# A graph attention and mixture-of-experts kernel: edges counted tile by tile, source one-hots begun on GpSimd, and other turns for weights, maxima and shifts

## The chip, the cores and the metric

The kernel runs on one core of a Trainium2 chip. The metric is the device time of one execution in microseconds. Engines are called by the profile's names: PE is TensorE (PEld its weight loads), DVE is VectorE, ACT ScalarE, POOL GpSimd, SP SyncE, which here only issues DMAs.

## The reference

1250 nodes of 768 values go through two graph attention layers, whose sum is added to x, and then through a mixture of eight experts with two chosen per node and a shared one. Edges are 21250 pairs (src, dst), sorted by dst; a self edge of each node is among them, and the reference adds one more.

```python
def _gat_layer(x, src, dst, W, a_src, a_dst, bias, concat):
    h = (x @ W).reshape(N, H, C)
    al_s = jnp.einsum('nhc,hc->nh', h, a_src)
    al_d = jnp.einsum('nhc,hc->nh', h, a_dst)
    e = jax.nn.leaky_relu(al_s[src] + al_d[dst], NEG_SLOPE)
    m = jax.ops.segment_max(e, dst, num_segments=N)
    ex = jnp.exp(e - m[dst])
    denom = jax.ops.segment_sum(ex, dst, num_segments=N)
    alpha = ex / (denom[dst] + 1e-16)
    out = jax.ops.segment_sum(h[src] * alpha[:, :, None], dst, num_segments=N)
...
x = x + gat(elu(gat(layernorm(x), W1, 4 heads of 512)), W2, 1 head of 768)
x = x + experts(layernorm(x))
```

## The kernel before

**Dense attention.** Edges are turned into a matrix of counts CT (1250 x 1250: how often src meets dst), kept as ten tiles of 125 sources. A softmax over edges is then one over a dense matrix: weight = count x exp(leaky(al_s + al_d) - shift), and aggregation is a matmul of h by these weights. Operands of the large matmuls are split in a high and a low 16-bit part (made by ScalarE and VectorE: `_hi` and `_lo`; GpSimd makes the low parts of W1 of head 0's last rows and of the experts), three products each.

**Stages**, each engine with its own hand-written order of instructions, held together by semaphores:

1. The x stage. VectorE turns src and dst into keys (chunk of dst, and source tile) that are laid out by four transposes on TensorE and copied to KEY and SLO (L1168, L1169). x comes in three pieces and is normalised (L1176 to L1193); TensorE transposes each of ten tiles (L1671), ScalarE and VectorE make its two parts (L896, L1220), and SyncE stores them to DRAM (xt_d), since SBUF holds three tiles only. W1's six row blocks for head 0 get their low parts at L1199.
2. The first projection (proj(0), L1654 in mm3): ten tiles of 18 matmuls. Each x tile is loaded back (L514). ScalarE copies a tile out of PSUM (L883), VectorE computes al_s and al_d from it (L1208) and the low part (L1213). Between the copies stand ScalarE's 32 sums for the second layer's attention vectors: GpSimd multiplies a block of W2's rows by att_src2 and att_dst2 (L774, two buffers) and ScalarE sums a product (L887, v2_sum). VectorE makes ten pieces of OL, the one-hots of sources within a tile (L1229, 2375 columns), in the same stretch. Then GpSimd works on W1 (L780, L781).
3. Counting (L1251 on VectorE, L1717 on TensorE). A loop of five turns, each with five chunks of 50 destinations: for every edge tile that may belong to a chunk VectorE makes a pair one-hot of 500 columns (12 buffers), and TensorE adds OL^T x one-hot into the chunk's PSUM bank; self edges are tiles of their own. 320 one-hots and matmuls. ScalarE copies each chunk to CT (L912). ScalarE also makes the high parts of head 1's W1 before its copies (L877). A total is checked at the end (L1259 to L1261); a wrong one would start a slow count of everything.
4. Masks: TensorE transposes CT's tiles (L1742), ScalarE turns counts into masks (two passes, L997 and L1000) and VectorE takes for every tile of destinations the maximum of al_s over its sources (L1299, chain_max); SyncE stores the masks (mask_d) for the later heads. The ten maxima become the softmax shifts (chain_shift: L1305 to L1309, a transpose on TensorE, L1698, a copy, L1314), go to DRAM (aa_d) and come back as rows. The first three tiles of the second projection are in this stage.
5. Four heads. Head h: the projection of head h+1 (ten tiles), then 15 groups: three blocks of destinations (500, 375, 375 columns), each with one denominator group and four aggregations (L1766, L1771), and for each the ELU and output (L1360 to L1386). A step of weights (p_steps) makes one source tile's weights in one block: ScalarE L925, L931, L943, VectorE L1320, L1328, L1335. Tables say how many steps stand in which tile of the projection (PJ_STEPS) and in which group (CUR_STEPS for this head, NEXT_STEPS for the next), where the ten maxima of the next head stand (MAX_STEPS), and where TensorE transposes and VectorE copies its shifts (SHIFT_AT). SyncE loads masks, W1 rows and x tiles for later heads in an order that is written out (L607 to L640).
6. The second layer, the router and the experts. GpSimd makes the low part of an expert's activations in three parts (L806); its down projection is L1654 in down().

```python
PJ_STEPS = [2, 1, 1, 0]
MAX_STEPS = [0, 0, 2, 2, 2, 2, 2, 0, 0, 0, 0, 0, 0, 0, 0]
ROW_AT, SHIFT_AT = 1, 8
```

## Time and profile before

| | us |
|---|---|
| median of 3 runs | 1466.32 |
| lowest and highest | 1466.25, 1472.4 |
| the profiled execution's own time | 1465.73 |
| its span in the trace | 1463.9 |
| TensorE busy | 1267.5 (87%) |
| VectorE busy | 931.5 (64%) |
| ScalarE busy | 595.6 (41%) |
| GpSimd busy | 257.6 (18%) |
| mean granted TensorE clock | 0.947 of full speed |

Busy is the time in which an engine executes; an engine may be idle or held for two reasons that this table doesn't tell apart, so the shares are to be read stage by stage. PE and DVE have 7118 and 1851 instructions in the trace. The largest group is TensorE's L1654 (projections and experts), 790.1 us busy.

### The profile page before, as it was taken

What the parts mean: (1) busy time and instruction counts of PE and PEld (TensorE: products, weight loads), DVE (VectorE), ACT (ScalarE), POOL (GpSimd) and SP (SyncE); (2) the same over time, 40 slices, a digit from 0 to 9 for tenths busy, and PEclk for the clock granted to TensorE, in tenths of its full rate; (3) what the DMA queues carried; (4) which work ended last, traced back from release to release, by engine and by line L of the source; (5) the groups of instructions that cost most, each with busy time, mean ns of one, the idle gap of its engine ahead of it and who ended that gap; (6) DMA issues with size and microseconds to landing.
All of it is one profiled execution on the core that took longest, in us unless ns stands there. A gap on an engine that the chain in (4) does not pass through costs nothing.

```text
span 1463.9 us, 19131 instructions
## 1 busy us (share of the span) xinstructions
PE 1267.5 (87%) x7118; PEld 814.8 (56%) x7118; DVE 931.5 (64%) x1851; ACT 595.6 (41%) x1025; POOL 257.6 (18%) x190
## 2 busy tenths in 40 slices
PE   1574898579599789979998999999999989999996
PEld 1342344334355455445456888888854746666664
DVE  6477997599788968988963456254478624333340
ACT  1344224566475546547842066200231134444441
POOL 1399300000000000000000000130011543443322
PEclk9987899899899989989998999999899989999999
DMA  8442201413441453114045611251310286767622
GB/s 209 153 161 76 78 0 34 144 51 95 114 131 38 113 157 90 40 36 117 30 134 187 187 58 57 75 149 32 97 66 1 62 240 175 187 174 173 164 58 29
DMA packets 71438, 152.66 MB, mean 104 GB/s; under 512 B 10837, under 2 KB 34901, under 8 KB 70730
## 3 DMA queue, kind: packets, MB, share of 16 engines
q1 hardware_dynamic: 64699, 134.28, 30.4%
q0 software_dynamic: 6656, 17.26, 6.1%
q8 instruction: 54, 0.88, 0.3%
q14 instruction: 29, 0.24, 0.1%
HBM read 118.93 MB, written 34.59 MB: 105 GB/s over the span
## 4 chain that ended last, share of the span: by engine, by line
PE 60%; DVE 17%; DMA 6%; ACT 6%; issue 5%; POOL 5%; SPq 1%; DVEq 0%; POOLq 0%; ACTq 0%
PE PS L1654 40%; PE PS L1771 10%; PE PS L1717 5%; DVE sb L1299 3%; POOL sb L774 3%; DVE sb L1320 2%; DVE sb L1328 2%; PE PS L1766 2%; DVE sb L1208 1%; DVE sb L1335 1%; DMA sb<-in_x_dram 1%; DVE sb L1251 1%; POOL sb L806 1%; DMA sb<-in_L_ffn_w_dram 1%; DVE sb L1371 1%
## 5 line engine op out<-in xcount | busy, mean ns | idle before, releaser
L1654 PE MATMUL PS<-sb,sb 128*125 128x384 f16 (+8 forms) x4404 | 790.1, 340 | 68.0 <-DVE sb L1213 23.4
L1654 PEld LDWEIGHTS PS<-sb,sb 128*125 128x125 f16 (+3 forms) x4404 | 543.7, 129 | 302.0 <-issue 70.7
L1771 PE MATMUL PS<-sb,sb 125*128 125x375 f16 (+1 forms) x1440 | 267.4, 347 | 0.0
L1771 PEld LDWEIGHTS PS<-sb,sb 125*128 125x128 f16 x1440 | 141.9, 99 | 121.9 <-issue 14.0
L786 POOL TENSOR_TENSOR sb<-sb,sb 125x768 f32<-125x768 f32 x10 | 18.0, 1841 | 784.4 <-DMA sb<-in_x_dram 784.4
L931 ACT ACTIVATE sb<-sb 125x375 f32<-125x375 f32 (+1 forms) x150 | 81.6, 544 | 116.1 <-DVE sb L1320 115.6
L1498 DVE SCALAR_TENSOR_TENSOR sb<-sb,sb 128x2304 f16<-128x2304 f32 x27 | 68.8, 2557 | 89.0 <-ACT sb L1066 89.0
L1717 PE MATMUL PS<-sb,sb 125*125 125x500 f16 x320 | 88.6, 417 | 12.6 <-DVE sb L1251 12.6
L1251 DVE TENSOR_SCALAR sb<-sb,sb 125x500 f16<-125x500 f16 x320 | 95.5, 380 | 3.3 <-PE PS L1717 3.2
L1320 DVE SCALAR_TENSOR_TENSOR sb<-sb,sb,sb 125x375 f32<-125x375 f32 (+1 forms) x150 | 95.3, 637 | 1.8 <-ACT sb L925 1.6
L925 ACT ACTIVATE sb<-sb,sb 125x375 f32<-125x375 f32 (+1 forms) x150 | 93.7, 628 | 3.9 <-DMA sb<-aa_d 3.9
L1208 DVE CUSTOM_DVE_ANT_0 sb<-PS,sb 125x512 f16<-125x512 f32 x80 | 55.2, 690 | 57.3 <-ACT sb L883 55.9
L1328 DVE SCALAR_TENSOR_TENSOR sb<-sb,sb 125x375 f32<-125x375 f32 (+1 forms) x150 | 87.6, 584 | 1.2 <-ACT sb L931 1.1
L1335 DVE TENSOR_TENSOR sb<-sb,sb 125x375 f16<-125x375 f32 (+1 forms) x150 | 87.8, 585 | 0.1
L774 POOL TENSOR_TENSOR sb<-sb,sb 128x768 f32<-128x768 f32 x32 | 77.9, 2469 | 55.6 <-DMA sb<-in_L_gnn_W_dram 46.6
L943 ACT ACTIVATE sb<-sb 125x375 f16<-125x375 f32 (+1 forms) x150 | 81.7, 545 | 8.5 <-DVE sb L1328 8.2
L1299 DVE CUSTOM_DVE_ANT_0 sb<-sb,sb 125x1250 bf16<-125x1250 bf16 x50 | 71.2, 1455 | 18.5 <-ACT sb L1000 10.0
L1717 PEld LDWEIGHTS PS<-sb,sb 125*125 x320 | 40.1, 141 | 60.9 <-issue 41.1
L806 POOL TENSOR_TENSOR sb<-sb,sb 128x392 f16<-128x392 f32 (+2 forms) x33 | 30.7, 931 | 203.3 <-ACT sb L1084 203.3
L1628 DVE TENSOR_TENSOR sb<-PS,sb 128x588 f16<-128x588 f32 x32 | 23.8, 767 | 66.5 <-ACT sb L1106 66.5
L1084 ACT ACTIVATE sb<-sb 128x392 f16<-128x392 f32 (+2 forms) x33 | 17.7, 536 | 108.6 <-DVE sb L1519 108.6
L968 ACT ACTIVATE sb<-sb,sb 128x375 f32<-128x375 f32 (+1 forms) x48 | 30.8, 641 | 69.7 <-DVE sb L1371 69.7
(190 smaller groups left out, 1122.8 us busy)
## 6 DMA issues: line engine op xcount, KB each, us to landing
sb<-in_L_ffn_w_dram SPq DMA_DIRECT2D x24, 1152.0 KB, 5.7
sb<-xt_d SPq DMA_DIRECT2D x40, 375.0 KB, 3.7
sb<-in_L_gnn_W_dram SPq DMA_DIRECT2D x32, 384.0 KB, 3.2
sb<-mask_d SPq DMA_DIRECT2D x20, 546.9 KB
sb<-h_d SPq DMA_DIRECT2D x10, 1000.0 KB, 5.5
h_d<-sb SPq DMA_DIRECT2D x16, 375.0 KB, 6.8
sb<-aa_d SPq DMA_DIRECT2D x5, 1093.8 KB
sb<-in_L_gnn_W_dram SPq DMA_DIRECT2D x18, 256.0 KB, 3.6
```

Of the source, the lines that this page charges most:

```text
L774: nc.gpsimd.tensor_tensor(VP[a][:, :], WV[ch % 3][:, :], A2R[:, a, :], ALU.mult).then_inc(s_vp, 1)
L925: A(TMP[:, q % NTMP, 0:n], ROW[:, 1, lo:lo + n], ACT.Identity, bias=ALF[:, h, i:i + 1]).then_inc(s_p1, 1)
L931: A(TMP[:, q % NTMP, 0:n], TMP[:, q % NTMP, 0:n], ACT.Exp).then_inc(s_p3, 1)
L943: A(P[:, i, 0, lo:lo + n], TMP[:, q % NTMP, 0:n], ACT.Copy).then_inc(s_p5, 1)
L1251: V.tensor_scalar(OR[:, n % RO, :], iok[:, :], 1000.0 * c, KEY[:, bass.ds(col, 1)], ALU.add, ALU.is_equal).then_inc(s_or, 1)
L1299: V.tensor_tensor_reduce(junk, mask, max_row(h), 1.0, 3.0 * NEG, ALU.add, ALU.max, MX[:, j:j + 1]).then_inc(s_mu, 1)
L1320: V.scalar_tensor_tensor(TMP[:, q % NTMP, 0:n], ROW[:, 0, lo:lo + n], AL[:, 0, h, i:i + 1], TMP[:, q % NTMP, 0:n], ALU.add, ALU.max).then_ ...
L1328: V.scalar_tensor_tensor(TMP[:, q % NTMP, 0:n], TMP[:, q % NTMP, 0:n], 1.0, CT[:, i, lo:lo + n], ALU.min, ALU.mult).then_inc(s_p4, 1)
L1335: V.tensor_tensor(P[:, i, 1, lo:lo + n], TMP[:, q % NTMP, 0:n], P[:, i, 0, lo:lo + n], ALU.subtract).then_inc(s_p6, 1)
L1654: ins = M(out_, lhs(a), rhs(b), start=first and a + b == 0, stop=last and a == 1)
L1717: ins = M(PS[0:T, c, 0:KC], OL[:, bass.ds(col, 1), :], OR[:, n % RO, :], start=q == 0, stop=q == len(jobs[c]) - 1)
L1771: ins = M(PS[:, t, 0:n], hb[:, i, pa, 128 * c:128 * c + 128], P[:, i, pb, lo:lo + n], start=i == 0 and pa + pb == 0, stop=i == NT - 1 and ...
```

## The change

- **Counting by tiles.** For each of the 170 edge tiles the one or two chunks that it may meet are listed (`met`); VectorE makes the one-hots for both in one operation of 500 or 1000 columns (170 of them), TensorE adds into four PSUM banks in turn (286 matmuls), with no loop. Self edges are no tiles any more: two VectorE operations add the identity to CT's diagonal blocks. 24 tiles (39 matmuls) are counted between the transposes of x. There are 8 one-hot buffers for 12.
- **Source one-hots.** GpSimd subtracts (ten operations of 2250 columns, the last of 1125, from 9.5 us on), VectorE compares with zero in place.
- **The products for W2's attention vectors** stand behind these: ten on GpSimd, then the low parts of W1, then 22 more; four buffers for two. ScalarE has six of the sums in the first projection, sixteen between chunk copies (three for four chunks) and ten in tile 3 of the second projection, all at once. The split of the sums (v2_split) moves to head 0's fifth group.
- **The first projection** takes x's tiles in the order 7, 8, 9, 0 to 6, and the first three aren't loaded back. The load of head 1's W1 rows is spread over this.
- **Masks** are made in one ScalarE pass; VectorE subtracts them.
- **The heads.** New tables: in heads 0 and 1 three steps of weights per group first, the ten maxima from group 5 to 9, the shifts at group 12 for 8; in head 2 shifts at 10. h1's stores stand ahead of the shift rows on SyncE, and one W1 load behind them.
- **Experts.** Each expert's first down projection waits part by part.

```diff
+    reach = [(max(0, c * DC * NE // N - MARGIN) // T, min(ET, -(-((c + 1) * DC * NE // N + MARGIN) // T)))
+             for c in range(NC)]
+    met = [[c for c in range(NC) if reach[c][0] <= t < reach[c][1]] for t in range(ET)]
+    assert all(1 <= len(m) <= 2 for m in met)
```
```diff
-        PJ_STEPS = [2, 1, 1, 0]
-        CUR_STEPS = [[3, 3, 2, 2, 2, 2, 2, 2, 0, 0, 0, 0, 0, 0, 0],
-                     [2, 2, 2, 2, 2, 2, 2, 0, 0, 0, 0, 0, 0, 0, 0],
-                     [2, 2, 2, 2, 2, 2, 2, 0, 0, 0, 0, 0, 0, 0, 0],
+        PJ_STEPS = [[0, 0, 0, 0, 2, 2, 2, 2, 2, 2], [1] * NT, [1] * NT]
+        CUR_STEPS = [[3, 3, 3, 3, 3, 2, 2, 1, 0, 0, 0, 0, 0, 0, 0],
+                     [3, 3, 3, 3, 3, 2, 2, 1, 0, 0, 0, 0, 0, 0, 0],
+                     [3, 3, 2, 2, 2, 2, 2, 2, 2, 0, 0, 0, 0, 0, 0],
                      [3, 3, 3, 3, 2, 2, 2, 0, 0, 0, 0, 0, 0, 0, 0]]
-        MAX_STEPS = [0, 0, 2, 2, 2, 2, 2, 0, 0, 0, 0, 0, 0, 0, 0]
-        NEXT_STEPS = [[0, 0, 0, 0, 0, 0, 0, 0, 0, 0, 1, 2, 2, 2, 2],
-                      [0, 0, 0, 0, 0, 0, 0, 0, 0, 0, 1, 2, 2, 2, 2],
-                      [0, 0, 0, 0, 0, 0, 0, 0, 0, 0, 2, 2, 3, 3, 3]]
+        MAX_STEPS = [[0, 0, 0, 0, 0, 2, 2, 2, 2, 2, 0, 0, 0, 0, 0],
+                     [0, 0, 0, 0, 0, 2, 2, 2, 2, 2, 0, 0, 0, 0, 0],
+                     [0, 0, 2, 2, 2, 2, 2, 0, 0, 0, 0, 0, 0, 0, 0]]
+        NEXT_STEPS = [[0, 0, 0, 0, 0, 0, 0, 0, 0, 0, 0, 0, 0, 0, 2],
+                      [0, 0, 0, 0, 0, 0, 0, 0, 0, 0, 0, 0, 0, 0, 2],
+                      [0, 0, 0, 0, 0, 0, 0, 0, 0, 0, 0, 3, 3, 3, 3]]
...
-        W1_AT = {3: 0, 4: 1, 5: 2, 6: 3, 7: 4, 8: 5}
-        ROW_AT, SHIFT_AT = 1, 8
+        W1_AT = {6: 0, 7: 1, 10: 2, 11: 3, 12: 4, 13: 5}
+        ROW_AT, SHIFT_AT = 1, [12, 12, 10]
```
SyncE, start and heads:
```diff
+            sp.wait_ge(s_xT, NT)
             sp.dma_start(A2R[:, 0, :], as2.to_broadcast([128, D])).then_inc(s_a2v, 16)
             sp.dma_start(A2R[:, 1, :], ad2.to_broadcast([128, D])).then_inc(s_a2v, 16)
-            for i in range(NT):
-                store_xt(i)
             for ch in range(3):
                 load_v2(ch)
-            for i in range(NT):
-                load_xt(0, i)
-                load_v2(3 + i)
-            for ch in range(3 + NT, NCH):
+            for q in range(3, NT):
+                load_xt(0, q)
+            load_w1_rows(1, range(2))
+            for ch in range(3, 8):
                 load_v2(ch)
+            load_al(1)
...
-            load_w1(1)
-            sp.wait_ge(s_vp, 2 * NCH)
             chain_row(0)
+            load_w1_rows(1, range(2, KD))
             for i in range(3):
                 load_xt(1, i)
+            for ch in range(8, NCH):
+                load_v2(ch)
...
                     load_masks(h + 1, 3)
                     load_masks(h + 1, 4)
+                    store_h1(NB * h)
                     if h + 2 < H:
-                        load_w1_rows(h + 2, range(2, KD))
+                        load_w1_rows(h + 2, range(2, 5))
                     chain_shift(h + 1)
+                    if h + 2 < H:
+                        load_w1_rows(h + 2, range(5, KD))
```
GpSimd and ScalarE:
```diff
+            pool.wait_ge(s_slo, 1)
+            for i in range(NT):
+                a, b = OLP * i, min(OLP * (i + 1), KA)
+                nc.gpsimd.tensor_tensor(OL[:, a:b, :], iot[:, :].unsqueeze(1).to_broadcast([T, b - a, T]),
+                                        SLO[:, a:b].unsqueeze(2).to_broadcast([T, b - a, T]), ALU.subtract
+                                        ).then_inc(s_od, 1)
...
+                        k = 2 * ch + a
+                        if k >= 4:
+                            pool.wait_ge(s_va, k - 3)
+                        nc.gpsimd.tensor_tensor(VP[k % 4][:, :], WV[ch % 3][:, :], A2R[:, a, :], ALU.mult
+                                                ).then_inc(s_vp, 1)
...
                 h_hi(0, i)
-                while k * NT < 2 * NCH * (i + 1):
-                    v2_sum(k)
-                    k += 1
-            act.sem_inc(s_ce, 1)
+                if i >= 4:
+                    v2_sum(summed)
+                    summed += 1
             w1_hi(1, range(KD))
...
+            for c in range(NC):
+                act.wait_ge(s_cm, reach[c][1])
+                A(CT[:, :, c * DC:c * DC + DC], PS[0:T, c % 4, 0:KC].rearrange("p (i n) -> p i n", n=DC), ACT.Copy,
+                  accum_out=CS[:, c:c + 1]).then_inc(s_ce, 1)
+                if c >= 4 and c % 4 < 3:
+                    v2_sum(summed)
+                    summed += 1
...
-                  ACT.Relu, bias=1.0, scale=-1.0).then_inc(s_act, 1)
-                act.wait_ge(s_act, j + 1)
-                A(MSK[:, j % 2, :], MSK[:, j % 2, :], ACT.Copy, scale=NEG).then_inc(s_mm, 1)
+                  ACT.Relu, bias=big[:, :], scale=NEG).then_inc(s_mm, 1)
...
+                        if h == 0 and i == NT // 3:
+                            for k in range(summed, 2 * NCH):
+                                v2_sum(k)
```
VectorE (the code of before at L1229 and L1251 is taken out):
```diff
+            def source_onehots(q):
+                a, b = OLP * q, min(OLP * (q + 1), KA)
+                dve.wait_ge(s_od, q + 1)
+                V.tensor_scalar(OL[:, a:b, :], OL[:, a:b, :], 0.0, None, ALU.is_equal).then_inc(s_ol, 1)
+
+            def pair_onehots(tiles):
+                for t in tiles:
+                    if t >= RO and t % RG == 0:
+                        dve.wait_ge(s_cm, t - RO + RG)
+                    c, w = met[t][0], len(met[t])
+                    V.tensor_scalar(OR[:, t % RO, 0:w, :], iok[:, 0:w, :], float(SP * c), KEY[:, t:t + 1], ALU.add,
+                                    ALU.is_equal).then_inc(s_or, 1)
+
+            piece(0)
+            piece(1)
+            for i in range(XF):
+                xt_lo(i)
+                if i < 2:
+                    source_onehots(i)
+                pair_onehots(range(T0 * i // XF, T0 * (i + 1) // XF))
+            piece(2)
+            for i in range(XF, NT):
+                xt_lo(i)
+
+            for q in range(NT):
+                h_lo(0, q)
+                if q >= 2:
+                    source_onehots(q)
...
+            pair_onehots(range(T0, ET))
+            dve.wait_ge(s_ce, NC)
...
+            flat = CT[:, :, :].rearrange("p i n -> p (i n)")
+            own = flat[:, 0:(NT - 1) * (N + T)].rearrange("p (i n) -> p i n", n=N + T)[:, :, 0:T]
+            V.tensor_tensor(own, own, idh[0:T, 0:T].unsqueeze(1).to_broadcast([T, NT - 1, T]), ALU.add
+                            ).then_inc(s_ctok, 1)
+            own = flat[:, (NT - 1) * (N + T):NT * N]
+            V.tensor_tensor(own, own, idh[0:T, 0:T], ALU.add).then_inc(s_ctok, 1)
```
TensorE:
```diff
+            def counts(tiles):
+                for t in tiles:
+                    if t % OLP == 0:
+                        pe.wait_ge(s_ol, t // OLP + 1)
+                    if t % PG == 0:
+                        pe.wait_ge(s_or, min(t + PG, ET))
+                    for w, c in enumerate(met[t]):
+                        if t == reach[c][0] and c >= 4:
+                            pe.wait_ge(s_ce, c - 3)
+                        ins = M(PS[0:T, c % 4, 0:KC], OL[:, t, :], OR[:, t % RO, w, :], start=t == reach[c][0],
+                                stop=t == reach[c][1] - 1)
+                    ins.then_inc(s_cm, 1)
+
+            def early(i):
+                return 2 * (T0 * i // XF // 2)
+
+            for i in range(XF):
+                x_T(i)
+                if i >= 2:
+                    counts(range(early(i - 2), early(i - 1)))
+            counts(range(early(XF - 2), T0))
+            for i in range(XF, NT):
+                x_T(i)
...
+            def down(lhs, wb, o_, made=None):
                 for q in range(2):
                     for m in range(KI):
+                        if made is not None and q == 0:
+                            pe.wait_ge(s_sg, made + KI)
+                            pe.wait_ge(s_alo, made + m + 1)
+                        elif made is not None:
+                            pe.wait_ge(s_gx, made + KI)
```

How the order of instructions changes, at three places. VectorE before, from SLO's copy to the first tile of the first projection (sb_52 is x, sb_190 and sb_191 its statistics, sb_69 the transposed x, sb_70 W1's parts, sb_51 is OL):

```order
L1169 COPY sb_149<-PS 125x170
...
L1193 TENSOR_SCALAR sb_52<-sb_52,sb_191,sb_165 125x768 x5
L1220 TENSOR_TENSOR sb_69<-PS,sb_69 128x750 x5
L1199 SCALAR_TENSOR_TENSOR sb_70<-sb_53,sb_70 128x512
L1220 TENSOR_TENSOR sb_69<-PS,sb_69 128x750
...
L1229 TENSOR_TENSOR sb_51<-sb_147,sb_149 125x2375
L1208 ISA sb_54,sb_156<-PS,sb_72 125x512
```

And with the change (x is sb_78, the transposed x sb_67, OL sb_51, the pair one-hots sb_59, W1 sb_68):

```order
L1188 COPY sb_153<-PS 125x170
L1189 COPY sb_152<-PS 125x170
...
L1214 TENSOR_SCALAR sb_78<-sb_78,sb_81,sb_169 125x768 x3
L1242 TENSOR_TENSOR sb_67<-PS,sb_67 128x750
L1251 TENSOR_SCALAR sb_51<-sb_51 125x2250
L1258 TENSOR_SCALAR sb_59<-sb_150,sb_152 125x500 x4
L1242 TENSOR_TENSOR sb_67<-PS,sb_67 128x750
L1251 TENSOR_SCALAR sb_51<-sb_51 125x2250
L1258 TENSOR_SCALAR sb_59<-sb_150,sb_152 125x1000 x5
...
L1258 TENSOR_SCALAR sb_59<-sb_150,sb_152 125x500
L1196 BN_STATS sb_80<-sb_78 125x6 x10
```

OL's compare has moved from the first projection between x's low parts, and pair one-hots stand behind it, ahead of x's last five tiles.

TensorE before, from x's transposes (L1671) to the row of al_s (L1694), with the loop of counting behind it:

```order
L1671 MATMUL PS<-sb_139,sb_52 128x125 x60
L1654 MATMUL PS<-sb_70,sb_69 125x512 x180
L1694 MATMUL PS<-sb_139,sb_156 10x125
L1708 UNCONDITIONAL_BRANCH
L1708 ISA
L1716 ISA
L1717 ISA
L1717 MATMUL PS<-sb_61,sb_51 125x500
```

And with the change (L1705 transposes, L1718 counts, L1688 projects, L1753 the row):

```order
L1705 MATMUL PS<-sb_143,sb_78 128x125 x18
L1718 MATMUL PS<-sb_59,sb_51 125x500 x4
L1705 MATMUL PS<-sb_143,sb_78 128x125 x6
L1718 MATMUL PS<-sb_59,sb_51 125x500 x8
L1705 MATMUL PS<-sb_143,sb_78 128x125 x6
L1718 MATMUL PS<-sb_59,sb_51 125x500 x27
L1705 MATMUL PS<-sb_143,sb_78 128x125 x30
L1688 MATMUL PS<-sb_68,sb_67 125x512 x180
L1753 MATMUL PS<-sb_143,sb_160 10x125
L1718 MATMUL PS<-sb_59,sb_51 125x500 x247
```

39 matmuls of counting have moved between the transposes, and 247 stand behind the projection.

SyncE in head 0 before, around the next head's shift rows (L560 and L566), with masks (L555), W1 (L481), h1 (L575) and x (L514):

```order
L481 DMA sb_71<-in_L_gnn_W_dram 128x512 x4
L560 DMA aa_d<-sb_162 20x125
L566 DMA sb_62<-aa_d 112x2500
L566 DMA sb_62<-aa_d 13x2500
L555 DMA sb_65<-mask_d 112x2x1250
L555 DMA sb_65<-mask_d 13x2x1250
L555 DMA sb_64<-mask_d 112x2x1250
L555 DMA sb_64<-mask_d 13x2x1250
L575 DMA h_d<-sb_75 128x4x500 x2
L514 DMA sb_69<-xt_d 128x1500 x3
L575 DMA h_d<-sb_76 128x3x500 x2
```

And with the change (shift rows L567 and L573, masks L562, W1 L490, h1 L582, x L519):

```order
L582 DMA h_d<-sb_73 128x4x500 x2
L490 DMA sb_69<-in_L_gnn_W_dram 128x512 x3
L567 DMA aa_d<-sb_166 20x125
L573 DMA sb_60<-aa_d 112x2500
L573 DMA sb_60<-aa_d 13x2500
L490 DMA sb_69<-in_L_gnn_W_dram 128x512
L562 DMA sb_63<-mask_d 112x2x1250
L562 DMA sb_63<-mask_d 13x2x1250
L562 DMA sb_62<-mask_d 112x2x1250
L562 DMA sb_62<-mask_d 13x2x1250
L519 DMA sb_67<-xt_d 128x1500 x3
L582 DMA h_d<-sb_74 128x3x500 x2
```

The first store pair of h1 stands ahead of the shift rows, and one W1 load behind them.

## Rows read from the trace of the kernel before

**Rows 1.** Windows of the whole run: stretch, us, busy (x) by engine, PEclk, DMA share, GB/s:
```profile
49.50:137.70 88.20, 49.23 (x180) 28.16 (x180) 57.05 (x61) 32.13 (x69) 74.78 (x31) 0.85 0.36 120
137.70:241.90 104.20, 89.31 (x323) 40.46 (x323) 97.58 (x329) 22.83 (x62) 19.44 (x14) 0.90 0.12 37
241.90:286.30 44.40, 29.62 (x188) 19.89 (x189) 24.11 (x50) 25.96 (x25) 0.00 (x0) 0.85 0.46 134
...
325.40:418.00 92.60, 76.90 (x419) 41.06 (x420) 82.75 (x144) 57.56 (x113) 0.00 (x0) 0.91 0.39 109
418.00:460.40 42.40, 40.36 (x181) 23.83 (x180) 36.23 (x79) 21.77 (x43) 0.00 (x0) 1.00 0.27 82
460.40:553.60 93.20, 81.55 (x447) 43.16 (x446) 77.42 (x134) 50.66 (x98) 0.00 (x0) 0.93 0.39 108
...
596.10:694.70 98.60, 86.45 (x468) 45.00 (x467) 84.16 (x148) 57.42 (x112) 0.00 (x0) 0.95 0.25 69
```

**Rows 2.** Timeline of PE, start, us, line, what, [idle before, releaser]: L1698:
```profile
381.07 0.38 PE L1698 MATMUL PS<-sb,sb 125*20 125x125 f32 x1 [15.70 <-DVE sb L1308]
...
516.05 0.38 PE L1698 MATMUL PS<-sb,sb 125*20 125x125 f32 x1 [11.63 <-DVE sb L1308]
```

**Rows 3.** Source view of L774, GpSimd's groups by form, VectorE's timeline at 8 us:
```profile
L774 POOL TENSOR_TENSOR sb<-sb,sb x26: 1794/1808/4202, 53.9 to 123.9; 128x768 f32<-128x768 f32 x26
...
L806 POOL TENSOR_TENSOR sb<-sb,sb 128x392 f16<-128x392 f32 x24 | 22.2, 926 | 118.0 <-ACT sb L1084 118.0
...
L781 POOL TENSOR_TENSOR sb<-sb,sb 128x512 f16<-128x512 f32 x6 | 6.9, 1152 | 0.5
...
9.47 0.34 DVE L1169 COPY sb<-PS 125x170 f32<-125x170 f32 x1
```

**Rows 4.** Source views of L1251 and L1489, and GpSimd in the timeline there:
```profile
L1251 DVE TENSOR_SCALAR sb<-sb,sb x3: 339/695/1892, 138.5 to 140.9; 125x500 f16<-125x500 f16 x3
...
139.01 1.85 POOL L774 TENSOR_TENSOR sb<-sb,sb 128x768 f32<-128x768 f32 x1
...
L1489 DVE TENSOR_SCALAR sb<-sb,sb,sb x10: 678/678/2198, 953.6 to 1047.1; 125x768 f32<-125x768 f32 x10
```

**Rows 5.** Timeline near 1145 us: one-hots on VectorE, additions on GpSimd:
```profile
1144.84 4.71 DVE L1602 TENSOR_SCALAR sb<-sb,sb 125x392 bf16<-125x392 f16 x20
...
1146.23 8.52 POOL L816 TENSOR_TENSOR sb<-sb,sb 125x768 f32<-125x768 f32 x3 [7.07 <-ACT sb L1097]
```

**Rows 6.** Groups by form in counting, 187 to 240 us:
```profile
L1251 DVE TENSOR_SCALAR sb<-sb,sb 125x500 f16<-125x500 f16 x191 | 49.8, 344 | 1.3 <-PE PS L1717 1.3
```

**Rows 7.** ScalarE: timeline of L877, and groups by form 50 to 131 us:
```profile
158.61 0.63 ACT L877 ACTIVATE sb<-sb 128x512 f16<-128x512 f32 x1 [2.19 <-DMA sb<-in_L_gnn_W_dram]
...
L887 ACT ACTIVATE sb<-sb 128x768 f32<-128x768 f32 x27 | 22.7, 842 | 33.0 <-POOL sb L774 33.0
```

**Rows 8.** VectorE's groups by form, 460 to 600 us (busy, mean ns, idle before):
```profile
L1208 DVE CUSTOM_DVE_ANT_0 sb<-PS,sb 125x512 f16<-125x512 f32 x22 | 15.2, 691 | 7.1 <-ACT sb L883 6.7
L1299 DVE CUSTOM_DVE_ANT_0 sb<-sb,sb 125x1250 bf16<-125x1250 bf16 x10 | 14.2, 1454 | 0.0
L1320 DVE SCALAR_TENSOR_TENSOR sb<-sb,sb,sb 125x375 f32<-125x375 f32 x21 | 12.4, 590 | 0.0
...
L1320 DVE SCALAR_TENSOR_TENSOR sb<-sb,sb,sb 125x500 f32<-125x500 f32 x10 | 7.2, 721 | 0.1
```

**Rows 9.** Head 1's shift rows and the x load behind: timeline and source L514:
```profile
523.67 0.27 DVE L1314 COPY sb<-PS 20x125 f32<-20x125 f32 x1
...
533.12 1.31 ACT L925 ACTIVATE sb<-sb,sb 125x500 f32<-125x500 f32 x2 [0.41 <-DMA sb<-aa_d]
...
L514 SPq DMA_DIRECT2D sb<-xt_d x1: 3196/3196/3196, 529.2 to 529.2; - x1
...
DMA to landing us min/median/max: 14.1/14.1/14.1
```

**Rows 10.** Timeline of PE, an expert's down projection:
```profile
1276.66 2.64 PE L1654 MATMUL PS<-sb,sb 128*98 128x384 f16 x15 [1.28 <-POOL sb L806]
```

265 lines of the change are left out of this document (109 added, 156 removed).

## The prediction

> **What bounds the kernel now.** I first cut the profiled execution into stages by a table of windows (core busy time per stretch), then read, for each stage, which wait ends last. The columns to compare are the length of a stretch with its TensorE busy time [rows 1]: the x stage ends at 49.5 us; the first head's projection takes 88.2 us for 49.2 us of TensorE work; counting and its check take 104.2 us; the mask stage up to the first weights 44.4 us; the attention of heads 0, 1 and 2 takes 92.6, 93.2 and 98.6 us. From counting on VectorE is as busy as TensorE in these stretches. The projection is slow because ScalarE's sums for W2 stand in its queue between the copies that free PSUM, behind GpSimd products of 1.8 us and their loads; counting is at VectorE's pace. Two of the attention stretches hold one gap each, where TensorE stands at the transpose of the next head's shifts until VectorE has made ten maxima: 15.7 and 11.6 us [rows 2].
>
> **The lock that the change leans on.** The change gives GpSimd ten differences of 2250 columns (the last 1125). GpSimd's tensor_tensor takes 1.80 us for 768 columns, 1.15 for 512 and 0.93 for 392 [rows 3], so 2.25 to 2.36 ns a column, and I take 5.1 us for 2250 (from 4.4, the slope between the 392 and 512 columns of its two 16-bit forms, up to 5.8). What this does to VectorE shows in three rows: while such an operation of 1.85 us runs, one of three pair one-hots takes 1892 ns, which are 344 on the mean elsewhere [rows 4, 6], and the operation that normalises a tile of 768 columns takes 2.20 us in one case of ten instead of 0.68 [rows 4]. So VectorE's SBUF-to-SBUF tensor_scalar waits until GpSimd's operation has ended. Conversely, twenty one-hots in a dense row (4.71 us) kept a GpSimd addition waiting: two additions, 3.6 us by their length [rows 3], took 6.75 [rows 5].
>
> **The x stage.** SLO is copied at 9.5 us [rows 3] and GpSimd starts. VectorE is then let in about once per GpSimd operation, with a group of adjacent instructions. I lay them out: the 2 normalisations (1.3 us) behind the first difference, 3 (2.0) behind the second, then source one-hots with 4 pair one-hots (1.8), with 5 (2.6), 5 (1.7), 5 (1.7), W1's low part with 5 (2.5), and the last 5 normalisations (3.0): 16.6 us in the port. 9.5 + 9.5 x 5.1 + 16.6 = 74.6; five more low parts of x and W1, two passes of about 0.69 [rows 8] together, give 82 us in place of 49.5: **+32.5**. The one-hots are priced from counting: 191 of 500 columns fill 49.8 us [rows 6], 0.26 each, where twenty of 392 columns take 0.235 each [rows 5]: 0.13 per 500 columns on a fixed 0.13, so 0.39 for 1000.
>
> **The first projection.** Nothing but six sums stands in it now; three tiles of x need no reload. A tile then takes 4.2 us (ten in 42.4 [rows 1]); with a slow first tile of 6 and 2.6 for the last copy and low part it ends at 82.3 + 6 + 9 x 4.25 + 2.6 = 129 instead of 137.7. The stage goes from 88.2 to 47.4: **-40.8**.
>
> **Counting.** The order shows a wait that counting did not have: ScalarE makes the high parts of W1 for head 1 before its first chunk copy, and TensorE, which has four banks, stops at tile 25 for that copy. Before, the last of these parts was made at 158.6 us [rows 7], 24 us after the projection, beside the first five chunks. GpSimd now also has a product to finish, and SyncE the row's round trip: I take 19.4 us from the end of the projection, nearly all with TensorE idle. Then 247 matmuls stay (286 in all, 39 early). TensorE needs some 0.2 us each (447 of 375 to 512 columns in 81.55 [rows 1]), 50 us. VectorE needs 101 x 0.39 for the tiles that meet two chunks and 45 x 0.26 for the rest, less 8 tiles that it makes ahead in the gap: 48. But sixteen W2 products of 1.8 us are tied in by ScalarE's sums, one for three chunks of four, and take the port; I let twelve to fifteen cost VectorE their length: 48 + 22 to 27 = 70 to 75, and take 70. The diagonal and the check I put at 4.4 us. 19.4 + 70 + 4.4 = 93.8 in place of 104.2: **-10.4**.
>
> The Trainium skill (SBUF — State Buffer, Who interferes with whom) says that whoever issues first holds the pair of ports that VectorE and GpSimd share for the whole instruction, and the other fully blocks. By that rule a GpSimd operation that is already queued goes ahead of VectorE's next one, and the sum would be rival (b)'s, 1467. Rows 4 agree with the blocking; rows 5, where GpSimd's operation waited through a row of one-hots, speak against the turns.
>
> **Masks and head 0.** One ScalarE pass per mask falls away. VectorE's ten maxima (1.45) and three tiles' low parts (three passes of 0.69) are 20.7 us [rows 8]; I take 24.5 from the transposes to the last maximum for 31.3: **-7**. Then ScalarE has ten sums of 842 ns [rows 7] behind six products of 1.8: about 12.9 us before the next copy out of PSUM. The wait for the shift rows, which was there anyway, covers about half: tile 4's copy comes 6 us later. The pipe of weights now fills only after it (2), and since tile 3 makes no steps any more the tenth tile's weights come two steps later (4): **+12**.
>
> **Attention, heads 0 and 1.** A step of weights on VectorE is three passes, 1.46 us in 375 columns and 1.85 in 500 (the first pass: 0.59 and 0.72), two maxima 2.8, a y about 1.7 [rows 8]. Three steps a group first, then maxima: the shifts are ready some 79 us after the projection in head 0 and 71 in head 1, and TensorE meets them at group 12, with 5 to 6 us of wait left and 3 us before the third block's weights. By adding groups: 83 us for 92.6 in head 0, **-9.6**, and 87.5 for 93.4 in head 1, **-5.9**. Head 2's projection runs its steps in 500 columns instead of 375, 0.3 us more a tile: **+1.8**, and so head 3's: **+1.8**.
>
> What is late next is a load. SyncE issues the x tiles of the projection after next behind the shift rows and two pairs of masks. After head 1's shift copy at 523.67 the first x tile was issued at 529.2 and took 14.1 us to land [rows 9], 19.6 us in all, with 1 MB of h1 ahead of it that the change moves away: about 16.5. The copy can only come once group 12 is read, 10.5 us before group 14 ends. So TensorE waits some 6 us for x before the projections of heads 2 and 3: **+12** together.
>
> **Head 2.** Its shifts move two groups, but its next head's weights can't start before the rows are back, 9.4 us after the copy (533.12 for 523.67 [rows 9]). With 20 own steps in nine groups VectorE ends these at 66 us; the copy follows group 10's reciprocal, 70; rows at 79.4; ten tiles' first weights take 28 us after that, as they did. Head 3's first denominator ends at 107.6 instead of 98.6: **+9**.
>
> **Experts.** TensorE waited 1.28 us at each expert's down projection for GpSimd's last low part [rows 10]; now the first two of three parts start before it, six matmuls, 1.0 us of cover, eight times: **-7.8**. The other moved loads, the h1 stores among them, cost nothing: SyncE reaches them while TensorE is in the same head's groups, and where that cover goes is the load wait above.
>
> **Sum.** +32.5 - 40.8 - 10.4 - 7 + 12 - 9.6 - 5.9 + 3.6 + 12 + 9 - 7.8 = -12.4. The span of 1463.9 becomes 1451.5, the execution's 1465.7 becomes 1453.3. The median shown is 0.6 above that execution, so I say **1454 us**.
>
> **The rivals.** (a) GpSimd's differences don't shut VectorE out: their 18 rows of 125 let it in between, or 16-bit columns go faster. For it: no row has such a form, and GpSimd's 1.5 us tensor_scalar let one-hots through. Against: rows 4. The x stage then ends at about 54 us: 1454 - 28 = 1426, and where also the products yield in counting (-15), 1411. (b) GpSimd and VectorE take turns instruction by instruction; the one-hots of 1892 and 695 ns [rows 4] can be read so. Then VectorE makes one instruction per difference, ten of some forty, and x ends at 95: 1454 + 13 = 1467, no change. This is what the rule of the Trainium skill told above would make of the stage. (c) Slower: the differences cost much more than 2.3 ns a column, for their broadcast rows. Each microsecond on each of them puts 9.5 us on the x stage, all of it on the path. From 7.2 us each it is slower by over 0.5%; at 8, 1454 + 28 = 1482. Nothing in the trace shows a broadcast on GpSimd. (d) The heads cost less than I add: x tiles land in time and head 2 is not held, 1454 - 21 = 1433.
>
> **Chances.** A difference of 0.5%, 7 us, is about what a measurement of this kernel can tell from none: the three runs span 6. My forecast 0.42, (a) 0.24, (b) 0.12, (c) 0.10, (d) 0.12. My own case lies within 15 us of 1454, mostly below 1459. Faster 0.72 (all of (a) and (d), most of mine), the same 0.15, slower 0.13. The range leaves out the far end of (a) and most of (c): **1410 to 1475**; the forecast's own is 1439 to 1469.
>
> **What would show it.** Right: TENSOR_TENSOR of 125x2250 on GpSimd near 5 us; a normalisation or one-hot of several microseconds in the x stage; its last low part near 82 us; TensorE idle some 18 us after tile 24, released by ScalarE's copy; 125x1000 one-hots at 0.39 pitch, and slower with a product beside them; the shift gaps down to about 5 us; a gap before the projections of heads 2 and 3 released by the x tile's load; a gap of about 16 us in head 3's first denominator; 32.1 us an expert instead of 33.1. Wrong: the x stage ending before 60 (then (a)) or after 100 ((c)); no load wait in the heads ((d)); counting at 50 us after its gap, which means that the products do not lock VectorE out.

## The result, and the profile after

The changed kernel takes 1473.41 us (median of 20 runs, 1466.82 to 1482.39) against 1466.74 of the kernel before (20 runs, 1464.29 to 1474.97): a ratio of 1.0038, 95% interval 1.0022 to 1.0055. That is 6.7 us slower, where I had forecast 1454, 12 us faster. It stays inside the half per cent that I had called the same (a chance of 0.15), and inside my range, but on the other side of the kernel before. The profiled execution took 1474.92 us, its span is 1473.2, the mean granted clock 0.933 (0.947 before). The experiments below were measured in three later series, each beside the kernel before, whose medians there were 1468.88, 1469.18 and 1470.85 us. A ratio in brackets is against the kernel before of the same series. "Less than the changed kernel" is a plain difference to 1473.41 from the first series, and leaves out this drift of 2 to 4 us. So small differences are read from stages of the traces instead.

This table of windows of the changed kernel has the columns of [rows 1]; its stretches are the same stages, cut where TensorE begins them:

```profile
0.00:79.30 79.30, 24.55 (x103) 17.24 (x103) 70.72 (x100) 12.68 (x20) 43.12 (x30) 0.92 0.46 121
79.30:123.20 43.90, 41.01 (x180) 25.37 (x180) 26.67 (x58) 11.95 (x24) 18.12 (x10) 0.95 0.54 164
123.20:145.30 22.10, 1.36 (x3) 0.37 (x3) 6.80 (x10) 3.08 (x7) 14.74 (x12) 0.52 0.52 155
145.30:223.90 78.60, 59.74 (x247) 34.64 (x247) 68.71 (x142) 29.10 (x80) 52.29 (x18) 0.91 0.13 40
223.90:251.30 27.40, 20.57 (x155) 15.40 (x155) 21.26 (x40) 14.32 (x13) 0.00 (x0) 0.81 0.52 149
251.30:310.20 58.90, 39.35 (x147) 21.06 (x148) 34.76 (x69) 35.01 (x65) 10.65 (x6) 0.82 0.28 80
310.20:397.20 87.00, 79.25 (x419) 41.62 (x417) 71.84 (x128) 45.52 (x92) 0.00 (x0) 0.93 0.31 85
397.20:403.50 6.30, 0.00 (x0) 0.00 (x0) 4.05 (x7) 4.88 (x10) 0.00 (x0) 0.78 1.05 274
403.50:455.70 52.20, 46.58 (x200) 26.82 (x201) 38.76 (x80) 23.41 (x42) 0.00 (x0) 0.96 0.27 86
455.70:543.90 88.20, 79.61 (x427) 41.74 (x425) 71.61 (x125) 45.31 (x91) 0.00 (x0) 0.94 0.32 84
543.90:550.90 7.00, 0.07 (x2) 0.05 (x1) 3.52 (x7) 4.54 (x9) 0.00 (x0) 0.76 1.04 278
550.90:603.00 52.10, 46.51 (x201) 26.65 (x202) 39.28 (x82) 23.98 (x44) 0.00 (x0) 0.96 0.28 81
603.00:704.40 101.40, 87.63 (x448) 42.85 (x447) 89.25 (x157) 63.67 (x126) 0.00 (x0) 0.89 0.23 68
...
781.00:1227.10 446.10, 424.24 (x2656) 325.06 (x2655) 227.91 (x526) 116.80 (x185) 65.66 (x47) 0.95 0.33 99
1227.10:1473.20 246.10, 232.59 (x1482) 157.46 (x1482) 80.89 (x68) 102.27 (x119) 91.92 (x77) 0.98 0.57 142
```

Measured against the stages of before, cut at the same instructions, in the order of the forecast's terms (stage before, after, difference, forecast):

| stage | before | after | moved | forecast |
|---|---|---|---|---|
| x stage | 49.5 | 79.3 | +29.8 | +32.5 |
| projection 0 | 88.2 | 43.9 | -44.3 | -40.8 |
| counting and check | 104.2 | 100.7 | -3.5 | -10.4 |
| masks to the shifts | 32.3 | 27.4 | -4.9 | -7 |
| to head 0's attention | 51.2 | 58.9 | +7.7 | +12 |
| attention 0 | 92.4 | 87.0 | -5.4 | -9.6 |
| waits for x, heads 2 and 3 | 0 | 13.3 | +13.3 | +12 |
| projection 2 and first denominator | 46.8 | 52.2 | +5.4 | +1.8 |
| attention 1 | 89.0 | 88.2 | -0.8 | -5.9 |
| projection 3 and first denominator | 46.9 | 52.1 | +5.2 | +1.8 |
| attention 2 and denominator 3 | 94.1 | 101.4 | +7.3 | +9 |
| head 3 | 76.4 | 76.6 | +0.2 | 0 |
| second layer, router | 439.3 | 446.1 | +6.8 | 0 |
| experts | 253.5 | 246.1 | -7.4 | -7.8 |

At the masks the changed kernel is 18.0 us ahead (223.9 for 241.9), as the forecast had it (18.7). It keeps that lead until the first wait for x, ahead of head 2's projection, and has lost it, and more, when the second layer begins (781.0 for 771.1).

### The profile page after: what moved, and what is told of

The parts are those of the page before. It is cut to its first block, busy times and chain, and to the rows that moved or that the text cites. A ratio compares the mean times of both kernels' runs of the same rounds, so it can differ in the third digit from the quotient of the medians.

```text
span 1473.2 us, 18197 instructions
## 1 busy us (share of the span) xinstructions
PE 1259.6 (86%) x7084; PEld 817.3 (55%) x7084; DVE 916.0 (62%) x1694; ACT 584.3 (40%) x1015; POOL 296.5 (20%) x198
## 4 chain that ended last, share of the span: by engine, by line
PE 52%; DVE 24%; ACT 6%; DMA 6%; issue 6%; POOL 5%; SPq 1%; POOLq 0%; DVEq 0%; ACTq 0%
PE PS L1688 39%; PE PS L1816 8%; DMA sb<-in_L_gnn_W_dram 3%; DVE sb L1258 3%; DVE sb L1230 3%; DVE sb L1352 3%; DVE sb L1331 3%; POOL sb L784 2%; DVE sb L1360 2%; DVE sb L1367 1%; DVE sb L1214 1%; DVE sb L1235 1%; ACT sb L965 1%; PE PS L1718 1%; DMA sb<-in_L_ffn_w_dram 1%
## 5 line engine op out<-in xcount | busy, mean ns | idle before, releaser
L1688 PE MATMUL PS<-sb,sb 128*125 128x384 f16 (+8 forms) x4404 | 789.5, 339 | 54.2 <-DVE sb L1235 17.3
L1688 PEld LDWEIGHTS PS<-sb,sb 128*125 128x125 f16 (+3 forms) x4404 | 545.0, 130 | 285.7 <-issue 68.4
L1816 PE MATMUL PS<-sb,sb 125*128 125x375 f16 (+1 forms) x1440 | 272.3, 351 | 0.0
L1352 DVE SCALAR_TENSOR_TENSOR sb<-sb,sb,sb 125x375 f32<-125x375 f32 (+1 forms) x150 | 95.9, 640 | 13.6 <-ACT sb L947 13.5
L1718 PE MATMUL PS<-sb,sb 125*125 125x500 f16 x286 | 70.5, 402 | 38.1 <-ACT sb L932 23.4
L1258 DVE TENSOR_SCALAR sb<-sb,sb 125x1000 f16<-125x1000 f16 (+1 forms) x170 | 81.4, 555 | 21.7 <-PE PS L1718 21.7
L1331 DVE CUSTOM_DVE_ANT_0 sb<-sb,sb 125x1250 bf16<-125x1250 f32 x50 | 71.2, 1456 | 14.5 <-ACT sb L1019 4.9
L1811 PE MATMUL PS<-sb,sb 125*128 125x375 f16 (+1 forms) x240 | 52.4, 362 | 30.3 <-DVE sb L1367 30.3
L1718 PEld LDWEIGHTS PS<-sb,sb 125*125 125x125 f16 x286 | 40.0, 146 | 67.3 <-ACT sb L932 24.6
L990 ACT ACTIVATE sb<-sb,sb 128x375 f32<-128x375 f32 (+1 forms) x48 | 30.8, 642 | 78.6 <-DVE sb L1403 78.6
```

What stands on the lines that cost most here:

```text
L1258: V.tensor_scalar(OR[:, t % RO, 0:w, :], iok[:, 0:w, :], float(SP * c), KEY[:, t:t + 1], ALU.add, ALU.is_equal).then_inc(s_or, 1)
L1331: V.tensor_tensor_reduce(junk, max_row(h), mask, 1.0, 3.0 * NEG, ALU.subtract, ALU.max, MX[:, j:j + 1]).then_inc(s_mu, 1)
L1352: V.scalar_tensor_tensor(TMP[:, q % NTMP, 0:n], ROW[:, 0, lo:lo + n], AL[:, 0, h, i:i + 1], TMP[:, q % NTMP, 0:n], ALU.add, ALU.max).then_ ...
L1688: ins = M(out_, lhs(a), rhs(b), start=first and a + b == 0, stop=last and a == 1)
L1718: ins = M(PS[0:T, c % 4, 0:KC], OL[:, t, :], OR[:, t % RO, w, :], start=t == reach[c][0], stop=t == reach[c][1] - 1)
L1816: ins = M(PS[:, t, 0:n], hb[:, i, pa, 128 * c:128 * c + 128], P[:, i, pb, lo:lo + n], start=i == 0 and pa + pb == 0, stop=i == NT - 1 and ...
```

## What the traces show of the two halves

**The x stage: turns, not groups.** GpSimd's ten differences, a source view, with minimum, median and maximum in ns:

```profile
L773 POOL TENSOR_TENSOR sb<-sb,sb x10: 2383/3944/4259, 9.5 to 45.9; 125x2250 f16<-125x2250 f16 x9, 125x1125 f16<-125x1125 f16 x1
```

And VectorE's timeline beside them (start, us, line, what):

```profile
13.96 3.44 DVE L1207 TENSOR_SCALAR sb<-sb 125x2 f32<-125x2 f32 x1
17.44 8.48 DVE L1214 TENSOR_SCALAR sb<-sb,sb,sb 125x768 f32<-125x768 f32 x2
25.84 2.85 DVE L1196 BATCH_NORM_STATS2 sb<-sb 125x6 f32<-125x384 f32 x6
...
33.69 12.70 DVE L1214 TENSOR_SCALAR sb<-sb,sb,sb 125x768 f32<-125x768 f32 x3
46.31 0.93 DVE L1242 TENSOR_TENSOR sb<-PS,sb 128x750 f16<-128x750 f32 x1
47.16 1.76 DVE L1251 TENSOR_SCALAR sb<-sb 125x2250 f16<-125x2250 f16 x1
48.84 1.12 DVE L1258 TENSOR_SCALAR sb<-sb,sb 125x500 f16<-125x500 f16 x4
```

The differences take 3.9 us on the median, 1.8 ns a column, less than even my lower bound of 4.4, and run without a break to 48.3 us. Each of VectorE's SBUF-to-SBUF tensor_scalars waits for one of them: even the one of two columns (L1207) takes 3.44, the two and three normalisations (L1214, 0.68 each when alone) 8.48 and 12.70. That is one operation to a difference. What doesn't wait is as plain: statistics (L1196, six in 2.85) and the low part that reads PSUM (L1242, 0.93) have their own length. From 48.8 us on four one-hots take 1.12 together. So the mechanism was rival (b)'s, and my layout in groups was wrong; the stage still ended near my 82 us only because two errors cancelled: the differences were shorter than I took them, and all of the one-hots came behind them. That is luck.

**Counting: the other way round.** The same two engines between 158 and 203 us; VectorE's row is its one-hots, GpSimd's a W2 product:

```profile
158.65 27.21 DVE L1258 TENSOR_SCALAR sb<-sb,sb 125x1000 f16<-125x1000 f16 x73
```

```profile
166.42 21.09 POOL L784 TENSOR_TENSOR sb<-sb,sb 128x768 f32<-128x768 f32 x1 [6.04 <-ACT sb L907]
```

Here VectorE's 73 one-hots ran in a dense row of 27.2 us, 0.37 each, the length that they have alone. One product, which takes 1.8 when alone, took 21.1 and ended 1.7 us after the row. Then it was ScalarE's turn to be late, and TensorE's (timelines; the brackets are idle time before, and the releaser):

```profile
187.54 0.84 ACT L907 ACTIVATE sb<-sb 128x768 f32<-128x768 f32 x1 [9.75 <-POOL sb L784]
```

```profile
145.34 8.99 PE L1718 MATMUL PS<-sb,sb 125*125 125x500 f16 x35 [19.18 <-ACT sb L932]
...
189.10 5.49 PE L1718 MATMUL PS<-sb,sb 125*125 125x500 f16 x17 [4.19 <-ACT sb L932]
```

ScalarE stood 9.75 us for that product with a chunk's copy behind it in its queue, and TensorE 4.2 us for the copy. Now the held products come at once, and the engines take turns again: between 190.6 and 202.4 us GpSimd made seven products and VectorE seven one-hots, one to one, in 12.1 us where such a row alone needs 2.7. The 19.18 us in the first PE row are the forecast's wait (19.4) for W1's high parts.

The Trainium skill (SBUF — State Buffer, Who interferes with whom) has the first to issue hold the shared ports for the whole instruction, where VectorE's operation needs both pairs. The trace agrees in the x stage, where each tensor_scalar waits out a difference. The same section lets an operation with one SBUF input, outside the modes that use both ports, run free, and the statistics agree. In counting the product was the one kept out, over dozens of VectorE's operations that were issued after it, and this the rule does not tell.

**The heads.** TensorE's timeline:

```profile
378.44 0.38 PE L1757 MATMUL PS<-sb,sb 125*20 125x125 f32 x1 [5.25 <-DVE sb L1340]
...
403.53 17.78 PE L1688 MATMUL PS<-sb,sb 128*125 128x512 f16 x72 [6.38 <-issue]
...
444.64 4.07 PE L1688 MATMUL PS<-sb,sb 128*125 128x512 f16 x18 [0.50 <-DVE sb L1235]
...
455.12 0.81 PE L1811 MATMUL PS<-sb,sb 125*128 125x500 f16 x2 [2.61 <-DVE sb L1367]
...
525.26 0.38 PE L1757 MATMUL PS<-sb,sb 125*20 125x125 f32 x1 [6.92 <-DVE sb L1340]
...
550.88 9.45 PE L1688 MATMUL PS<-sb,sb 128*125 128x512 f16 x35 [6.93 <-issue]
```

The waits at the shifts (L1757) fell from 15.7 and 11.6 us [rows 2] to 5.3 and 6.9, and that of head 2, 8.8 us in the trace of before, is gone. In their place stand 6.4 and 6.9 us ahead of the projections, a pause of 0.50 in nearly every tile (before, the last six tiles of a projection ran without one), and 2.6 us inside the first denominator, whose last weights come out of that projection. In head 2 the next head's first denominator trickles in one pair of matmuls at a time; one of its waits:

```profile
688.40 0.60 PE L1811 MATMUL PS<-sb,sb 125*128 125x500 f16 x2 [1.67 <-DVE sb L1367]
```

The experts do as forecast, 0.40 where there were 1.28 [rows 10], in 32.21 us each for 33.12:

```profile
1259.33 2.12 PE L1688 MATMUL PS<-sb,sb 128*98 128x384 f16 x12 [0.40 <-POOL sb L821]
```

## The experiments

**heads_before** and **heads_alone** split the change in two.

```diff
-        PJ_STEPS = [[0, 0, 0, 0, 2, 2, 2, 2, 2, 2], [1] * NT, [1] * NT]
+        PJ_STEPS = [[2] * NT, [1] * NT, [1] * NT]
...
-        ROW_AT, SHIFT_AT = 1, [12, 12, 10]
+        ROW_AT, SHIFT_AT = 1, [8, 8, 8]
...
-                        load_w1_rows(h + 2, range(2, 5))
+                        load_w1_rows(h + 2, range(2, KD))
                     chain_shift(h + 1)
```

(all five tables are as before, the sixth W1 row is no longer loaded behind the shift rows, and store_h1 stands behind the shift rows and ahead of the x loads, as before; heads_alone puts the same difference the other way into the kernel before, except for head 0's steps in tile 3 of its projection)

> The changed kernel with the five step tables, the shift groups and SyncE's order in the heads as before; counting, masks, projection order and experts stay changed. Theory A: the start gains (223.9 for 241.9 us at the masks, 251.3 for 274.2 at head 0's shifts) and the experts gain 7.4; what is lost lies in the heads from the second projection's end to head 3's first denominator, where the new turns cost 25 us in all (att of head 0 +0.8, projections +5.4 and +5.2, head 1 +6.2, head 2 +7.2). So about 1474 - 25 = 1449, below the kernel before by 17. Rival B: the heads are slower because the start leaves something behind them (a lower granted clock, 0.933 for 0.947; late sums), whatever the tables: then 1468 to 1474.

> The kernel before with only the new step tables, shift groups and SyncE's order in the heads. Theory A: slower than before by about 25 us, 1491, with a gap of 6 to 7 us before the projections of heads 2 and 3, 4.56 us for most tiles in them, and a slower head 2. Rival B: within 3 us of before.

Measured: heads_before 1456.25 us (ratio 0.9908, interval 0.9874 to 0.9942), heads_alone 1490.04 (1.0151, 1.01 to 1.0202). The new turns, with SyncE's new order, are what loses: 17 us from one side (25 were expected), 21 from the other. Rival B is out, since the old turns are 17 us faster behind the very same start, at the same clock (0.935). In heads_before TensorE has the old picture, no pause in the last six tiles and the long waits at the shifts:

```profile
368.11 0.38 PE L1753 MATMUL PS<-sb,sb 125*20 125x125 f32 x1 [16.27 <-DVE sb L1336]
...
423.99 25.07 PE L1684 MATMUL PS<-sb,sb 128*125 128x512 f16 x108 [0.37 <-DVE sb L1231]
```

and in heads_alone the new one:

```profile
416.33 18.75 PE L1658 MATMUL PS<-sb,sb 128*125 128x512 f16 x72 [6.72 <-issue]
...
468.88 0.60 PE L1770 MATMUL PS<-sb,sb 125*128 125x500 f16 x2 [2.61 <-DVE sb L1339]
```

**x_first** and **x_w1_first** mend SyncE's order.

```diff
                     store_h1(NB * h)
                     if h + 2 < H:
-                        load_w1_rows(h + 2, range(2, 5))
+                        for i in range(3):
+                            load_xt(h + 2, i)
+                        load_w1_rows(h + 2, range(2, KD))
                     chain_shift(h + 1)
-                    if h + 2 < H:
-                        load_w1_rows(h + 2, range(5, KD))
```

(x_w1_first; x_first moves the x tiles alone; in both the x tiles' old load, further down, is taken out)

> The changed kernel, with the three x tiles that SyncE loads behind the shift rows and two pairs of masks issued ahead of the W1 rows and the shift rows instead. Theory A: the two gaps before the projections of heads 2 and 3 (6.4 and 6.9 us, named issue in the trace) go, and with them the low clock at each projection's start: 13 to 15 us less, 1459 to 1461. Rival C: the gaps have another cause that stands behind the same load (ScalarE's W1 part behind the shift rows, whose wait of 4.4 us is in the same place): then 2 us or less.

> As x_first (1461.95), and W1's sixth row block is loaded ahead of the shift rows too, where the kernel before had it. Theory A: in x_first the gap before the projections of heads 2 and 3 shrank from 6.4 and 6.9 us to 1.8 and 1.2, released by VectorE's last low part of W1, whose load came late, and ScalarE stood 3.8 us for that load; both go: 3 to 6 us less, 1456 to 1459, and so within 3 us of heads_before (1456.25), which means that the new turns are worth nothing in heads 0 and 1 even with their loads in time. Rival I: the tables were only spoiled by the two loads: below 1452.

Measured: x_first 1461.95 (0.9953, 0.993 to 0.9975), 11.5 less than the changed kernel; x_w1_first 1458.59 (0.9893, 0.9838 to 0.9947), 3.4 less again. In x_first the wait before head 2's projection is down to 1.8 us and has another releaser, VectorE's low part of W1, behind a ScalarE that waits for the row's load:

```profile
404.56 7.98 PE L1687 MATMUL PS<-sb,sb 128*125 128x512 f16 x36 [1.81 <-DVE sb L1219]
```

```profile
403.16 0.63 ACT L895 ACTIVATE sb<-sb 128x512 f16<-128x512 f32 x1 [3.83 <-DMA sb<-in_L_gnn_W_dram]
```

In x_w1_first that is gone too. Whether it is worth 3.4 us isn't shown. From the transpose of head 0's shifts to the first matmul of the second layer the changed kernel's trace has 529.7 us, x_first 513.1, x_w1_first 514.1 and heads_before 509.9. In another place the same code differs by more: counting behind its first wait took 84.9 us in x_first's trace and 79.1 in x_w1_first's.

These stretches say what the new turns lose: of the 19.8 us between the changed kernel and heads_before the two late loads make 15.6, and the tables themselves 4.2. The tables do gain where they were meant to: with the loads in time attention 0 takes 86.4 us for heads_before's 94.7, and attention 1 88.1 for 89.8. They lose 5.0 and 3.3 in the projections of heads 2 and 3 with their first denominators, and 6.5 behind these. Rival I, below 1452, isn't borne out, though one of the four runs took 1450.61 and the interval reaches below it.

**max_early** asks whether the place of the maxima makes the wait at the shifts.

```diff
-        MAX_STEPS = [[0, 0, 0, 0, 0, 2, 2, 2, 2, 2, 0, 0, 0, 0, 0],
-                     [0, 0, 0, 0, 0, 2, 2, 2, 2, 2, 0, 0, 0, 0, 0],
+        MAX_STEPS = [[0, 0, 2, 2, 2, 2, 2, 0, 0, 0, 0, 0, 0, 0, 0],
+                     [0, 0, 2, 2, 2, 2, 2, 0, 0, 0, 0, 0, 0, 0, 0],
```

> The changed kernel with the next head's maxima in groups 2 to 6 instead of 5 to 9 in heads 0 and 1; steps and shift group stay. Theory A: TensorE's wait at the shifts (5.3 and 6.9 us) is not there because the maxima are late as such but because VectorE has 28 steps, ten maxima and the outputs of eight groups ahead of group 12 and is paced by ScalarE in the groups with maxima. With the maxima earlier the shifts are ready before group 12 but the own weights of blocks two and three come later: the wait moves to their denominators and the time stays within 4 us. Rival G: the maxima's place alone makes the wait; it goes and 10 us with it, 1463.

Measured: 1471.88 (1.0023, 1.0003 to 1.0042), within 2 us of the changed kernel. The wait at the shifts is gone in both heads. In head 0 the third block's denominator has two waits of 3.2 us instead, and the x load comes no earlier:

```profile
370.89 0.81 PE L1811 MATMUL PS<-sb,sb 125*128 125x375 f16 x2 [3.17 <-DVE sb L1367]
...
378.99 0.27 PE L1757 MATMUL PS<-sb,sb 125*20 125x125 f32 x1
...
402.77 18.22 PE L1688 MATMUL PS<-sb,sb 128*125 128x512 f16 x72 [7.63 <-issue]
```

The wait moves to the denominators, as Theory A has it, and Rival G's 10 us are not there. But the place of the maxima isn't without effect. Attention 0 and 1 take 84.5 and 84.0 us here, for 87.0 and 88.2 in the changed kernel's trace, and the waits for x behind them grow from 6.4 and 6.9 us to 7.6 and 9.1. So half of the 6.7 us gained goes into the late load, which hides it from the total.

**w1_later** takes the wait ahead of counting.

```diff
-            w1_hi(1, range(KD))
...
                   accum_out=CS[:, c:c + 1]).then_inc(s_ce, 1)
+                if c < KD:
+                    w1_hi(1, (c,))
```

> The changed kernel with ScalarE's six high parts of head 1's W1 each behind one of the first six chunk copies, not all ahead of the first. Theory A: TensorE's 19.2 us wait at tile 25 goes, but VectorE's one-hots then meet GpSimd's six low parts (1.17 us each) as well as the products, and VectorE sets the pace: 8 to 12 us less, 1462 to 1466. Rival D: counting is bound by the sums and products in ScalarE's queue, so that the wait only moves to a later chunk: 3 us or less.

Measured: 1464.31 (0.9972, 0.9949 to 0.9994), 9.1 less, so Rival D falls. In the traces the masks begin 5.5 us earlier (218.4 for 223.9) and the second layer 6.2; the rest lies where the code is the same. The wait of 19.2 us is gone from tile 25; the longest in counting is now this, where a chunk's copy stands behind a W1 row that is still being loaded:

```profile
149.83 7.67 PE L1718 MATMUL PS<-sb,sb 125*125 125x500 f16 x21 [7.66 <-ACT sb L930]
```

**ol_dve** and **diff_small** are about the differences.

```diff
-                V.tensor_scalar(OL[:, a:b, :], OL[:, a:b, :], 0.0, None, ALU.is_equal).then_inc(s_ol, 1)
+                V.tensor_tensor(OL[:, a:b, :], iot[:, :].unsqueeze(1).to_broadcast([T, b - a, T]),
+                                SLO[:, a:b].unsqueeze(2).to_broadcast([T, b - a, T]), ALU.is_equal
+                                ).then_inc(s_ol, 1)
```

(ol_dve; GpSimd's ten subtractions are taken out)

> The changed kernel without GpSimd's ten differences: VectorE makes the source one-hots itself in one operation (2.6 us for 2375 columns in the kernel before) in the places where it now compares with zero. Theory A, the lock: the x stage ends near 62 us for 79, the first projection gets 5 us longer because eight of the longer operations stand in it (2.1 + 2.5 us of VectorE a tile), the sum is 10 to 13 us less, 1461 to 1464. Rival E: the differences cost VectorE nothing and the x stage is long for its own one-hots: then the stage ends near 84 and the time goes up by 5.

```diff
+                for lo in range(a, b, 6):
+                    hi = min(lo + 6, b)
+                    ins = nc.gpsimd.tensor_tensor(OL[:, lo:hi, :], iot[:, :].unsqueeze(1).to_broadcast([T, hi - lo, T]),
...
+                ins.then_inc(s_od, 1)
```

(diff_small; the operation over all columns is taken out)

> The changed kernel with each of GpSimd's ten differences cut into three of 750 columns (the same columns in all). Theory J, turns: between 9.5 and 48.3 us VectorE got one SBUF tensor_scalar in for each of the ten differences, so with 29 shorter ones it gets three times the turns: its 9 early operations are through at about 9.5 + 9 x 1.4 + their own length = 28 us, TensorE's transposes start by 16 and 20 us, and the x stage ends 15 to 20 us earlier, near 62: 1455 to 1459. Theory A of the forecast, groups: VectorE takes all that stands ready whenever GpSimd ends an operation, so the number of operations matters as well, but it would have been through with 9 in five turns: 3 to 8 us less. Rival K: GpSimd keeps the port until its queue is empty, whatever the cut: no change, 1473.

Measured: ol_dve 1454.99 (0.9898, 0.9851 to 0.9946), 18.4 less; diff_small 1470.88 (1.0002, 0.9978 to 1.0025), 2.5 less, or 5 by the ratios, whose intervals just touch. In ol_dve the transposes start at 13.45 us and the projection at 57.7 for 79.35; its tiles wait 0.41 for the longer operation of VectorE:

```profile
13.45 2.76 PE L1701 MATMUL PS<-sb,sb 125*128 125x125 f32 x12 [4.59 <-DVE sb L1208]
...
57.70 25.69 PE L1684 MATMUL PS<-sb,sb 128*125 128x512 f16 x108 [2.46 <-DVE sb L1214]
...
97.09 4.07 PE L1684 MATMUL PS<-sb,sb 128*125 128x512 f16 x18 [0.41 <-DVE sb L1229]
```

```profile
L1245 DVE TENSOR_TENSOR sb<-sb,sb 125x2250 f16<-125x2250 f16 x9 | 25.5, 2830 | 0.0
```

Rival E falls. The 21.6 us that the x stage gives are more than my 17, and the projection pays about 7 of them back; at the masks ol_dve is 14.7 us ahead (209.3 for 223.9). The rest of the 18.4 isn't placed. diff_small shows the turns operation by operation, and that I had overrated them:

```profile
14.14 3.46 DVE L1216 TENSOR_SCALAR sb<-sb,sb,sb 125x768 f32<-125x768 f32 x2
...
30.15 5.85 DVE L1260 TENSOR_SCALAR sb<-sb,sb 125x500 f16<-125x500 f16 x4
...
37.81 7.94 DVE L1260 TENSOR_SCALAR sb<-sb,sb 125x1000 f16<-125x1000 f16 x5
```

Its transposes begin at 15.95 and 17.66 us, as turns foretold (16 and 20). But the one-hots, which had stood behind the last difference, now stand beside the differences, and each took a turn as well: four in 5.85 us and five in 7.94, which need 1.12 and 2.03 otherwise. GpSimd's 29 pieces end at 54.0 us, the projection begins at 76.8, 2.6 us earlier. What VectorE gains by shorter turns it pays by more of them. Rival K's reason is out, since the transposes did start earlier; of theory J only the mechanism holds. The total can't tell these 2.6 us: in this trace counting behind its first wait took 85.0 us for 78.6, with the same code.

**small_products** cuts the products of W2.

```diff
-                        nc.gpsimd.tensor_tensor(VP[k % 4][:, :], WV[ch % 3][:, :], A2R[:, a, :], ALU.mult
+                        w = D if k < 4 else 8
+                        nc.gpsimd.tensor_tensor(VP[k % 4][:, 0:w], WV[ch % 3][:, 0:w], A2R[:, a, 0:w], ALU.mult
```

(the scale of ScalarE's sums is set to 1 as well)

> The changed kernel with 28 of GpSimd's 32 products cut to 8 columns and the sums unscaled (it leaves out the attention vectors of the second layer). The sums stay in ScalarE's queue with their length. Theory A: the sixteen products in counting shut VectorE out for 1.8 us each; without them counting after TensorE's first wait falls from 74.4 to about 53 us, and tile 3 of the second projection waits 8.3 us less little: in all 18 to 24 us less, 1450 to 1456. Rival F: one-hots go on beside the products, counting is paced by the one-hots' own length: 5 us less at most.

Measured: 1443.78 (0.983, 0.9785 to 0.9876), 29.6 less than the changed kernel, more than expected. Rival F falls. TensorE counts without a break:

```profile
144.49 53.83 PE L1719 MATMUL PS<-sb,sb 125*125 125x500 f16 x245 [17.72 <-ACT sb L933]
```

So the 74.4 us of counting after the first wait hold 20.6 that the products make. How they divide shows in VectorE's one-hots, by form, here and then in the changed kernel:

```profile
L1259 DVE TENSOR_SCALAR sb<-sb,sb 125x1000 f16<-125x1000 f16 x96 | 41.0, 485 | 15.9 <-PE PS L1719 15.9
L1259 DVE TENSOR_SCALAR sb<-sb,sb 125x500 f16<-125x500 f16 x42 | 12.6, 346 | 0.6 <-PE PS L1719 0.6
...
L1258 DVE TENSOR_SCALAR sb<-sb,sb 125x1000 f16<-125x1000 f16 x96 | 51.4, 597 | 21.4 <-PE PS L1718 21.4
L1258 DVE TENSOR_SCALAR sb<-sb,sb 125x500 f16<-125x500 f16 x42 | 18.8, 490 | 0.2 <-PE PS L1718 0.2
```

The same 138 one-hots are busy for 53.6 us here and 70.2 there: 16.6 us are turns that VectorE waited. The 4.2 us of the late copy make up the rest.

**heads_before_w1** and **three_undone** put together what had lost.

> Heads as before and ScalarE's W1 parts behind the first chunk copies: the sum of two runs that took 17 and 9 us from the changed kernel. Theory A: the two lie in different stages and add: 1447. Rival: the earlier start of the masks only waits for a load there: 1453 or more.

> Heads as before, W1's high parts behind the chunk copies, source one-hots by VectorE: of the change there stay the counting by tiles, the projection that doesn't reload three tiles, the sums out of the projection, the masks in one pass and the experts' partial waits. The first two gave 1444.5, the third took 18 us by itself from the changed kernel. If they add: 1426 to 1428. Rival: with the x stage shorter, counting starts while the W1 rows are still loading and the gain shrinks: 1435.

Measured: heads_before_w1 1444.46 (0.9832, 0.9786 to 0.9879) and three_undone 1430.75 (0.9704, 0.9646 to 0.9762). The first is 11.8 below heads_before, so its Rival falls. The second is 13.7 below the first, and lies between its Theory (1426 to 1428) and its Rival (1435). Its four runs span 14.8 us (1424.13 to 1438.9), so the median decides nothing. The traces show that most adds up: the masks begin 13.5 us earlier than in heads_before_w1 (205.0 for 218.5), where ol_dve had 14.7. three_undone is 40 us faster than the kernel before in the same series (1470.85): the counting by tiles, the short projection, the single mask pass and the experts' split are worth that once GpSimd's differences, the W1 parts ahead of the first copy and the new turns are left out.

## Why the prediction was wrong

**What held.** That TensorE idles ahead of counting for W1's parts (19.2 us), the x loads (13.3 for 12), head 2 (7.3 for 9), the experts (7.4 for 7.8), and that the differences shut VectorE out: without them the masks begin 14.7 us earlier. Start to masks came to 18.0 for 18.7, but that is luck in part: the x stage and its projection were better than forecast by 6.2 us, counting worse by 6.9. In the projection the slow first tile that I had priced didn't come.

**What failed.** Four terms miss by 30 us together; the x stage with its projection (6.2 us better than forecast), the way to head 0's attention (4.3 better) and smaller ones bring it to the 22 us between the forecast (-12.4) and the span (+9.3):

- *Attention 0 and 1 (-9.6 and -5.9), which came to -5.4 and -0.8: 9.3 us.* I added groups as if three steps a group and then maxima ran at VectorE's busy time. In three of the groups with maxima VectorE waits 1.17 us for ScalarE inside the output, where no step of weights is left to fill it, and once for a W1 part, 1.7 us in head 0 and 1.6 in head 1 (VectorE's timeline in head 0):

```profile
360.08 0.69 DVE L1220 SCALAR_TENSOR_TENSOR sb<-sb,sb 128x512 f16<-128x512 f32 x1 [1.73 <-ACT sb L896]
...
362.41 0.55 DVE L1410 SCALAR_TENSOR_TENSOR sb<-sb,sb 128x375 f32<-128x375 f32 x1 [1.17 <-ACT sb L992]
```

That is some 5 us a head. In max_early, whose maxima stand among the steps, the two attentions are 2.5 and 4.2 us shorter than in the changed kernel.

- *Projections 2 and 3 (+1.8 each), which came to +5.4 and +5.2: 7 us.* The 0.3 a tile was right in kind (4.56 a tile for 4.15), but it holds for six tiles (2.6), and I had left out that the first denominator then waits for the last tile's weights: 2.6 us at its last pair.
- *Counting (-10.4), which came to -3.5: 6.9 us.* From the end of the projection to the end of TensorE's wait passed 22.1 us for 19.4: the wait itself is 19.2, and I had left nothing for what comes ahead of it. Counting behind it took 74.4 us for 70, the check 4.2 for 4.4. The products cost 20.6 us, near my 22, but the base was too low: without them small_products needs 53.8 us for my 48 to 50. The price was right by luck in part, as 4.2 of the 20.6 are the copy behind ScalarE's sum, which was in no step of mine, though [rows 5] show the starving. A single trace doesn't settle the miss: with the same code this stretch, check included, took 78.6 us in the changed kernel's trace and 85.0 in diff_small's.
- *The second layer (0), which came to +6.8.* No code there was changed but the experts. Cut at the very first matmul of the first down projection, six of which now stand ahead of the wait, it took 439.3 us before and 443.1 here: 3.0 of the 6.8 come from where the table cuts. The other 3.8 lie within what the traces of the other kernels have with the same code, 438 to 446, so they can be the scatter of single executions. In this trace a W2 load came later (TensorE's wait near the stage's start 4.7 for 2.2 us), and the granted clock was 0.89 in the 60 us before 1073, where before had 0.93 in the 58 us before 1058. The cause stays open.

**The rivals.** (a) fell: the differences shut VectorE out. (b) was the mechanism, with another time, as its 5.1 us were too long. (c) had the right sign and the wrong reason: differences cheaper than I thought. (d) fell. None of them doubted that the new turns gain in attention 0 and 1. Yet the forecast's own terms for the heads add up to a loss of 9.1 us (-9.6 - 5.9 + 3.6 + 12 + 9); it came to 25.0, and heads_alone is 21 us slower by itself. A forecast that already has a part of the change losing is a reason to leave that part out.

**Slips in the sums.** The projection's terms add up to 46.9 us, not 47.4. Head 1's attention is 93.2 us in [rows 1], not 93.4. W1's last part at 158.6 us is 20.9 behind the projection's boundary at 137.7, not 24. None of them changes the forecast by 1 us.

## What to carry to other kernels

A wait that vanishes at one place is only gained if nothing behind it was waiting too. Here the waits at the shifts shrank, and TensorE stood before the next projection instead, for a load that the new order had made late: with both loads in time 15.6 of the 19.8 us came back. So ask of a new order what each load now stands behind, and count the small waits inside a unit of work, not its busy time. Before work goes to a helper engine, look whether it shares a port with the one it relieves, and who stands in a queue behind its result.

## What the runs showed of the hardware

- A GpSimd tensor_tensor over 2250 16-bit columns with two broadcast operands took 3.9 us on the median and 4.3 at most, beside VectorE's work: 1.8 ns a column, where the 32-bit form of 768 columns takes 2.35.
- Beside unbroken GpSimd work each of VectorE's SBUF-to-SBUF tensor_scalars in a row waited for one GpSimd operation, even one of two columns (3.44 us), while statistics (six in 2.85) and an operation that reads PSUM (0.93) ran at their own length. In counting it was seven one-hots to seven products.
- Beside an unbroken row of 73 one-hots on VectorE one GpSimd product of 1.8 us took 21.1 us. In both stretches the engine that already ran without a break went on, and the other waited; the reason isn't shown.
